# Window attention, 32 images on one core: both scaled key copies from one spread of the norms

## The reference

```
xw = windows(roll(group_norm(x)))           # 8 x 8 pixel windows, 64 tokens of 64 channels
q, k, v = split(xw @ qkv_w + qkv_b)         # 4 heads of 16 channels
scores = q @ k.T / max(|q| * |k|, 1e-6)     # cosine attention: a norm per token and head
scores = scores / clip(tau, 0.01)           # one tau per head
attn = softmax(scores + bias + mask)
out = attn @ v @ proj_w + proj_b
skip = x + layer_norm(out)
```

## Time and profile before

| What | Value |
|---|---|
| Median of the runs | 838.54 us |
| The profiled execution | 839.52 us |
| Its span, first to last instruction | 837.7 us |
| TensorE busy (PE) | 718.8 us, 86% |
| VectorE busy (DVE) | 518.8 us, 62% |
| ScalarE busy (ACT) | 488.4 us, 58% |
| GpSimd busy (POOL) | 373.9 us, 45% |
| Mean granted TensorE clock | 0.913 |
| The two matmul groups of the first spread, lines 507 and 509 | 64 instructions each |
| The second spread, line 518 | 64 instructions |

### The profile page before, as it was taken

One profiled execution on the slowest core, in us unless ns is written; L12 is line 12 of the kernel. 1 busy time (PEld: TensorE's weight loads), 2 busy tenths in 40 slices (PEclk: granted clock), 3 DMA queues, 4 the chain that ended last, 5 costly groups with the idle time before them and its releaser, 6 DMA issues. The chain is left out here.

```text
span 837.7 us, 21571 instructions
## 1 busy us (share of the span) xinstructions
PE 718.8 (86%) x8482; PEld 385.6 (46%) x8482; DVE 518.8 (62%) x964; ACT 488.4 (58%) x986; POOL 373.9 (45%) x464
## 2 busy tenths in 40 slices
PE   4784799999999999999998489999999648659587
PEld 3562455555555555555554132333333228644264
DVE  4791367767776676777776112777777857661155
ACT  3663366777777777777775368877777117733000
POOL 4696356677767677667766220022222233300000
PEclk9775599999999999999999879999999758969889
DMA  9630000000000000000000020221111212000478
GB/s 211 149 87 11 1 2 2 2 3 2 2 2 3 2 3 3 2 2 2 3 2 3 0 51 1 49 50 46 45 43 49 76 43 54 0 1 1 57 165 268
DMA packets 15436, 31.38 MB, mean 37 GB/s; under 512 B 7208, under 2 KB 9004, under 8 KB 15340
## 3 DMA queue, kind: packets, MB, share of 16 engines
q1 hardware_dynamic: 14216, 29.61, 14.5%
q10 hardware_dynamic: 856, 0.20, 0.2%
q0 software_dynamic: 272, 0.27, 0.2%
HBM read 20.70 MB, written 9.37 MB: 36 GB/s over the span
## 5 line engine op out<-in xcount | busy, mean ns | idle before, releaser
L757 POOL TENSOR_TENSOR sc<-sc,mx 128x512 f32<-128x512 f32 x128 | 133.6, 1044 | 34.2 <-DVE mx L705 34.2
L702 DVE TENSOR_TENSOR sc<-s_ps,bias_tab 128x512 f32<-128x512 f32 x128 | 87.7, 685 | 58.9 <-PE s_ps L532 58.9
L655 ACT ACTIVATE pt<-t_ps 128x512 f32<-128x512 f32 x128 | 75.9, 593 | 52.6 <-PE t_ps L543 51.4
L1199 POOL TENSOR_TENSOR square<-xs 128x1024 f32<-128x1024 f32 x16 | 33.8, 2110 | 162.2 <-DVE xs L1101 162.2
L705 DVE TENSOR_REDUCE mx<-sc 128x8 f32<-128x512 f32 x128 | 87.8, 686 | 4.4
L1018 ACT ACTIVATE hs<-h_ps,fb1s 128x512 f32<-128x512 f32 x128 | 78.1, 688 | 17.6 <-PE h_ps L932 17.5
L543 PEld LDWEIGHTS t_ps<-consts,sc 128*128 128x128 f32 x512 | 53.7, 141 | 73.1 <-issue 45.8
L543 PE MATMUL t_ps<-consts,sc 128*128 128x128 f32 x512 | 83.9, 286 | 2.2 <-ACT pt L655 1.6
L532 PE MATMUL s_ps<-kx,qu 32*64 32x128 f32 x2048 | 71.4, 276 | 1.5 <-DVE sc L702 1.4
L932 PE MATMUL h_ps<-xs,fw 64*128 64x512 f32 x256 | 68.4, 648 | 1.0 <-ACT hs L1018 1.0
L945 PE MATMUL c_ps<-hs,fw 128*64 128x512 f32 x256 | 62.0, 604 | 0.8 <-DVE fcsq L1045 0.7
(11 more groups left out here) (190 smaller groups left out, 1393.2 us busy)
## 6 DMA issues: line engine op xcount, KB each, us to landing
raw<-in_x_dram SPq DMA_DIRECT2D x32, 256.0 KB, 5.1
xr<-in_x_dram SPq DMA_DIRECT2D x32, 256.0 KB, 4.1
out_dram<-x SPq DMA_DIRECT2D x32, 256.0 KB, 3.8
rec_scratch<-r SPq DMA_DIRECT2D x4, 224.0 KB, 4.5
xs<-rec_scratch SPq DMA_DIRECT2D x4, 224.0 KB
w<-in_L_conv_W_dram SPq DMA_DIRECT2D x1, 784.0 KB
w<-in_L_conv_W_dram SPq DMA_DIRECT2D x1, 672.0 KB
consts<-in_c_consts_dram SPq DMA_DIRECT2D x1, 400.0 KB, 4.0
```

Source lines behind the costliest of these rows:

```text
L655: act.activation(pt[a][2 * hp + j][:, :, :], t_ps[:, :, :], ACT.Exp).then_inc(s["exped"], 1)
L702: dve.tensor_tensor(sc[n % KEPT][:, :, :, :], s_ps[j][:, :, :, :], bias_tab[:, j, hp], ALU.add)\
L757: pool.tensor_tensor(v, v, mx[n % KEPT][:, :].unsqueeze(2).broadcast_to([128, 8, TOK]), ALU.subtract)\
```

## The change

Both key copies are now made from one spread. `spread_keys` keeps one form with all heads, times 1/tau. A new small constant `parity`, two columns, holds 1 on the partitions of even heads in its first column and 1 on those of odd heads in its second; it is computed in the preparation by two reductions of the identity matrix. `scale_keys` becomes a `scalar_tensor_tensor`: keys times the column times the spread norm. All four key scales of a pair stand together in `vector_step`, ahead of the query scales. `spread_second` and its semaphore are gone. The first spread signals twice, once when `a_ps` is there and once when `b_ps` is. `project_heads` waits for `keys_odd` instead of `keys_even`. `project_keys` waits for `proj_out` too.

```diff
-        spread_keys = sb(attention, "spread_keys", [128, 2, 128])
+        spread_keys = sb(attention, "spread_keys", [128, 128])
+        parity = sb(attention, "parity", [128, 2])
...
-                        for h, spread in enumerate((spread_even, spread_odd)):
-                            last = dve.tensor_scalar(spread_keys[:, h], spread, tau_sb[:, 0:1], None, ALU.mult)
-                        link(last)
+                        link(dve.tensor_scalar(spread_keys[:, :], spread_all, tau_sb[:, 0:1], None, ALU.mult))
+                        link(dve.tensor_reduce(heads_of[:, :], ident.rearrange("c (m d) -> c m d", d=DH), X, ALU.add))
+                        link(dve.tensor_reduce(parity[:, :], heads_of[:, :].rearrange("c (g h) -> c h g", h=2), X, ALU.add))
...
                     after(pe, s["keys_odd"], 2 * p)
+                    after(pe, s["proj_out"], 2 * (p - 3) + 2)
                     project(pe, a_ps, wk, p, "k_ps")
...
                     for a in range(2):
-                        pe.matmul(a_ps[a][:, :], spread_keys[rows(a), 0], rn[rows(a), :], start=True, stop=True)
+                        last = pe.matmul(a_ps[a][:, :], spread_keys[rows(a)], rn[rows(a), :], start=True, stop=True)
+                    last.then_inc(s["first_spread"], 1)
                     for a in range(2):
                         last = pe.matmul(b_ps[a][:, :], spread_all[rows(2 + a)], rn[rows(2 + a), :], start=True, stop=True)
                     last.then_inc(s["first_spread"], 1)
-
-            def spread_second(pe, p):
-
-                if there(p, PAIRS):
-                    pe.wait_ge(s["keys_even"], 2 * p + 2)
-                    after(pe, s["proj_out"], 2 * (p - 2) + 2)
-                    for a in range(2):
-                        last = pe.matmul(a_ps[a][:, :], spread_keys[rows(a), 1], rn[rows(a), :], start=True, stop=True)
-                    last.then_inc(s["second_spread"], 1)
...
                     if there(p + 2, PAIRS):
-                        pe.wait_ge(s["keys_even"], 2 * (p + 2) + 2)
+                        pe.wait_ge(s["keys_odd"], 2 * (p + 2) + 2)
...
                     act.wait_ge(s["norm_ps"], p + 1)
-                    after(act, s["second_spread"], p)
+                    after(act, s["first_spread"], 2 * p)
...
-                    dve.wait_ge(s[("first_spread", "second_spread")[h]], p + 1)
+                    dve.wait_ge(s["first_spread"], 2 * p + 1)
                     after(dve, s["scores"], 4 * (p - 2) + 2 * a + 2)
-                    dve.tensor_tensor(kx[p % 2][a][:, h], a_ps[a][:, :], k_sb[a][:, :], ALU.mult)\
+                    dve.scalar_tensor_tensor(kx[p % 2][a][:, h], k_sb[a][:, :], parity[:, h:h + 1], a_ps[a][:, :],
+                                             ALU.mult, ALU.mult)\
                        .then_inc(s[("keys_even", "keys_odd")[h]], 1)
...
-                spread_second(pe, n - 1)
                 turn(pe, n - 2, 6)
...
                 scale_keys(dve, n, 0, 0)
+                scale_keys(dve, n, 0, 1)
                 scale_keys(dve, n, 1, 0)
+                scale_keys(dve, n, 1, 1)
                 scale_queries(dve, n, 0)
                 scale_queries(dve, n, 1)
                 bias_max(dve, n - 1, 6)
                 bias_max(dve, n - 1, 7)
                 divide(dve, n - 1, 0)
-                scale_keys(dve, n, 0, 1)
-                scale_keys(dve, n, 1, 1)
```

More of the change, by code:

```diff
@@ L252, in build @@
             small = sb(stage, "small", [128, 2])
+            heads_of = sb(stage, "heads_of", [128, 2 * HEADS])
             tau_sb = sb(stage, "tau_sb", [128, 1])
@@ L335, in weights_there @@
                 eng.wait_ge(w_in, 16 * len(loads))
-            WP_READY = 10
+            WP_READY = 12
             def prepare_tensor(pe):
@@ L426, in build @@
                 "k_ps", "q_ps", "k_out", "q_out", "k_sq", "q_sq", "norm_ps", "norm_ln", "rnorm", "first_spread",
-                "second_spread", "keys_even", "keys_odd", "queries", "v_ps", "v_out", "scores", "biased", "row_max",
+                "keys_even", "keys_odd", "queries", "v_ps", "v_out", "scores", "biased", "row_max",
                 "shifted", "turned", "exped", "mixed", "sum_ln", "sum_recip", "heads", "proj_ps", "proj_out", "csq",
@@ L718, in scale_queries @@
                 if there(p, PAIRS):
-                    dve.wait_ge(s["first_spread"], p + 1)
+                    dve.wait_ge(s["first_spread"], 2 * p + 2)
                     after(dve, s["scores"], 4 * (p - 2) + 2 * a + 2)
```

## The result

The changed kernel takes 865.55 us (median of 4 runs, 862.89 to 868.35) against 838.36 us before; the ratio is 1.0316 with a 95% interval of 1.0282 to 1.0351. It is slower, as forecast, but by 27.2 us where 17.4 were forecast, and above the range of 845 to 861. A second set of runs of the same kernel gave 865.47 (1.0318, 1.0275 to 1.036). Times of different sets of runs differ by a microsecond or two; the kernel before was timed in each, at 838.4 to 839.4.

The account below looks back on a forecast made before the run. TensorE, busy 22.95 of 23.35 us a step, was taken to set the pace, with the changed key scales closing a loop. Loop and first steps, 17.1 us, plus preparation, 0.3, on the median gave 855.9 us; range 845 to 861.

Parts of the forecast that it names:

- The heads' projection is held by the key scales, and that closes a loop.: Attention stage: projection waits for VectorE's odd key scales, starts 1.39 us later; steps become 24.46 us instead of 23.35.
- the forecast of slower: Whole kernel: the change makes it slower, chance 0.91.
- 1.06 us removed are worth 0.28.: TensorE, second spread: of 1.06 us removed per pair only 0.28 is a gain; the ScalarE and GpSimd chain is late next.
- The new form costs 0.055 more from start to start.: VectorE key scales: scalar_tensor_tensor starts lie 0.655 us apart, against 0.60 for plain products.
- the figure of 21 us: Upper bound of the added time, if each key scale began only when the one before had ended, 0.74 us apart.
- Fourteen steps of 1.11, 0.83 in step 2, 0.70 in step 1.: Attention stage: steps 3 to 16 pay 1.11 us each, steps 2 and 1 wait for scaled queries; sum 17.1 us.
- The clock as a rival with a chance of 0.05.: TensorE in the stage: clock falls to 0.95 on average, 15 us more, 871; chance 0.05 shared with another late chain.
- The range.: Kernel time: 845 to 861 us, from the half loop to a little above the held scales; the loop's own 852 to 860.

Follow-up runs that it names:

- e4_late: The kernel before, second spread kept, with two more unused 512-column products on VectorE right before the even key scales: 858.15 us (1.0214).
- e7_back: The changed kernel with one idle matmul where the second spread stood, behind the mixing, in steps 3 to 16: 862.9 us (1.0278).
- e2_filler: The changed kernel with one idle 512-column matmul on TensorE in front of the heads' projection in steps 3 to 16: 861.92 us (1.0265).
- e5_filler1: The changed kernel with the idle matmuls of e2_filler and two more behind the first spread of step 1: 853.76 us (1.017).

## Why the prediction was right and wrong

- *The heads' projection is held by the key scales, and that closes a loop.* Right. Forecast 24.46 a step and 1.39 later; measured 24.45, and e4_late shows the loop without any of the rest. So the forecast of slower stands on the right mechanism and not on luck.
- *1.06 us removed are worth 0.28.* Right: 5.30 from projection to variances in e4_late, 5.01 in the changed kernel. A filler of 0.96 us put in its place costs nothing (e7_back), so most of the work was indeed hidden.
- *The new form costs 0.055 more from start to start.* Right: 2.71 against 2.48 for four, and 24.45 against 24.22 a step. One takes 0.74 and four together 2.71, so they lie (2.71 - 0.74) / 3 = 0.66 apart, each starting before the one before has ended. The Trainium skill, "VectorE: DVE Perf Modes", section "The DRAIN you can't avoid", says that the next operation doesn't start until the pipeline is empty, which the prediction drew on, and adds in the same paragraph that an operation that isn't held starts earlier. The trace agrees with this addition, which the prediction left out; the section doesn't speak for the figure of 21 us.
- *Fourteen steps of 1.11, 0.83 in step 2, 0.70 in step 1.* The waits are about right (0.59 in step 1 by itself), and step 2 grew by 1.2. The length of step 1 is wrong: 2.9 more, because the clock came up later in both profiles. It need not: e7_back has 0.5.
- *The clock as a rival with a chance of 0.05.* This is the step that failed: the sum has no term for the clock, so new waits of TensorE were priced at nothing but their own length. I argued from the drain, where the clock stands at 1.00 over 20 us with gaps under 1 us, and from a single group of matmuls of full length behind a gap of 2.19. Neither carries that far. The changed kernel's first profile has the same gap of 2.19 at the same place of the drain and a slow group behind it, its second the gap and a group of full length (1.09 at 493.53). And the drain's gaps of 0.78 and 0.86 have slow matmuls behind them in seven of eleven profiles.

```profile
494.95 1.23 PE L602 MATMUL b_ps<-rv,consts 32*128 32x512 f32 x4 [2.19 <-DVE ob L724]
496.12 1.98 PE L578 MATMUL a_ps<-ob,wp 64*64 64x512 f32 x8
```

  The waits that I had computed myself, 1.39 in each step and 3.9 us less the old work in step 1, were longer than any in the old loop. In the two profiles the clock costs 5.4 and 4.0 us in steps 4 to 15, 2.2 and 2.3 in step 1 and about 1 each in step 16 and the drain, 8.6 and 7.3 in all. The spans miss the forecast by 11.5 and 6.5 us; what is left lies in the start (1.7 and 0.5 over the forecast), in the stages behind, which didn't change (1.0 and -1.4), and 0.1 or 0.2 elsewhere. That the waits in the loop cause the falls is shown by e2_filler; that the wait in step 1 causes the late rise is not. The price I had given that rival, 15 us by a mean clock of 0.95 over the stage, was too high for the loop: the clock over 200 to 400 us of the span is 0.98. The Trainium skill, "TensorE: Matmul & The Clock Gate", section "A second HAM failure mode: psum-queue depth-cycling", says that frequent short idles can make the clock swing between its levels. This case agrees: with waits of 1.33 us, and two shorter ones behind, it swung in 3 or 4 of 12 steps. I had let two stretches of one profile overrule that.
- *The range.* Its bounds were those of the loop, 852 to 860, and it ended one microsecond above them. With the 7.3 to 8.6 us that the clock cost, the sum of 855.9 becomes 863 to 865.

## What to carry to other kernels

Before an operation is made longer or moved, look at how closely the next engine's wait for it is met: 0.18 us of slack on a shared bank turned 1.4 us on an engine that was 72% busy into 1.1 us on every step. When a forecast adds waits to TensorE, price the clock as a term of the sum, and not by one stretch that stayed at full clock: the same waits can be followed by slow matmuls in the next execution. And look at the first steps, where the clock is still low, by themselves. When a removed operation gives nothing back, try the order: here a loop was closed by what stood in front of the projection, and opening it was worth more than the operation.

## What the runs showed of the hardware

A wait of 1.09 us per step never lowered TensorE's clock in twenty-four steps, one of 1.33 did so in eleven of thirty-six, one of 1.93 in seven of twelve. But the length of one wait isn't all: behind 0.78 and 0.86 us, two waits close together in step 17, it fell in seven of eleven profiles. In the loop each fall cost 1.34 us in the changed kernel and 1.53 in e7_back, where a matmul stood in the place of the two waits for GpSimd. In step 17 of e2_filler and e5_filler1 it cost 2.4 and 2.5. At the start of the stage one filled wait (e5_filler1) moved a step from 24.7 (e2_filler) to 18.3 us. Which steps fall differs between executions of the same program; why it is every third or fourth is open.
